# Graph attention on one core: VectorE's adds set singly between its other operations, registers loaded for 16 tiles, two quads weighted in any round, chunks of five at the end

## The reference, cut to what matters

```python
def _gatv2_layer(x, src, dst, edge_e, Wl, bl, Wr, br, att_w, bias):
    gl = (x @ Wl + bl).reshape(n, HEADS, CH)          # 4 heads of 32 channels
    gr = (x @ Wr + br).reshape(n, HEADS, CH)
    xj = gl[src]
    e = jax.nn.leaky_relu(xj + gr[dst] + edge_e, negative_slope=0.2)
    alpha = jnp.einsum('ehc,hc->eh', e, att_w)
    m = jax.ops.segment_max(alpha, dst, num_segments=n)
    alpha = jnp.exp(alpha - m[dst])
    denom = jax.ops.segment_sum(alpha, dst, num_segments=n)
    alpha = alpha / (denom[dst] + 1e-16)
    out = jax.ops.segment_sum(xj * alpha[..., None], dst, num_segments=n)
    return out.reshape(n, HEADS * CH) + bias
```

## Time and profile before

| | us |
|---|---|
| median of 3 runs | 7069.02 (7065.85 to 7079.0) |
| the profiled execution | 7070.88 |
| its span | 7069.1 |
| PE busy | 5523.2 (78%) |
| DVE busy | 4561.9 (65%) |
| POOL busy | 4643.2 (66%) |
| ACT busy | 2511.6 (36%) |
| mean granted clock of TensorE, as a share of 2.4 GHz | 0.901 |

### The profile page before, as it was taken

The page is one execution under the profiler, slowest core; times in us unless marked ns, Lnnn a source line. Parts: engine busy times, 40 slices in busy tenths (PEclk is TensorE's granted clock), DMA queues, the critical chain, the costliest instruction groups (busy, mean ns, idle before and its releaser), DMA issues.

```text
span 7069.1 us, 115934 instructions
## 1 busy us (share of the span) xinstructions
PE 5523.2 (78%) x33353; PEld 4640.2 (66%) x33353; DVE 4561.9 (65%) x15147; ACT 2511.6 (36%) x9678; POOL 4643.2 (66%) x4865
## 2 busy tenths in 40 slices
PE   7988871888888888788867878757877866888875
PEld 6655551787876587777556667656766765767764
DVE  5434321677676488777657777756777765777775
ACT  2554420777775387777401111110111111111111
POOL 1777776777774377777247777727777745777770
PEclk9999999999998599999679998978899987998986
DMA  3111112444443255444234444434444443444441
GB/s 105 42 41 36 40 23 67 130 125 128 125 128 80 73 154 149 145 146 140 41 103 137 138 133 138 132 58 134 135 136 134 138 93 95 138 136 135 138 129 22
DMA packets 396212, 763.44 MB, mean 108 GB/s; under 512 B 110888, under 2 KB 255133, under 8 KB 394825
## 3 DMA queue, kind: packets, MB, share of 16 engines
q0 software_dynamic: 180928, 315.57, 19.1%
q1 hardware_dynamic: 210314, 426.15, 17.9%
q10 hardware_dynamic: 4352, 14.30, 0.7%
HBM read 648.79 MB, written 106.03 MB: 107 GB/s over the span
## 4 chain that ended last, share of the span: by engine, by line
POOL 25%; DVE 11%; issue 11%; PE 10%; DMA 5%; DVEq 2%; ACT 1%; POOLq 0%; ACTq 0%
POOL AR L565 19%; POOL AR L557 6%; DMA AR<-gtab_d,AR 4%; PE PS L1313 3%; PE PS L1329 2%; DVE AR L1934 2%; PE PS L1326 2%; DVE AR L1950 2%; DMA AR<-ptab_d,AR 1%; DVE AR L1960 1%; DVEq L491 1%; DVE AR L1792 1%; DVEq L1934 1%; PE PS L1227 0%; DVE AR L1717 0%
## 5 line engine op out<-in xcount | busy, mean ns | idle before, releaser
L565 POOL DMA_INDIRECT AR<-gtab_d,AR x2436 | 2302.6, 945 | 1183.0 <-issue 706.9
L557 POOL DMA_INDIRECT AR<-ptab_d,AR x1624 | 1541.6, 949 | 684.9 <-issue 470.9
L1329 PE MATMUL PS<-AR,ident 128*128 128x140 f32 x4872 | 1199.4, 331 | 537.6 <-DMA AR<-gtab_d,AR 526.9
L1329 PEld LDWEIGHTS PS<-AR,ident 128*128 128x128 f32 x4872 | 849.6, 214 | 730.4 <-DMA AR<-gtab_d,AR 720.4
L1326 PE MATMUL PS<-AR 128*128 x4872 | 1108.0, 313 | 50.0 <-issue 49.3
L1934 DVE TENSOR_TENSOR AR<-AR,PS 112x132 f32 x2436 | 709.0, 291 | 579.1 <-DVE AR L1934 325.5
L542 POOL DMA_INDIRECT rec_d<-AR x782 | 790.0, 1010 | 387.9 <-issue 234.5
L1227 PE MATMUL PS<-AR,ident 128*128 128x160 f32 x3248 | 782.8, 323 | 268.0 <-DMA AR<-ptab_d,AR 263.3
L1326 PEld LDWEIGHTS PS<-AR 128*128 128x128 f32 x4872 | 858.5, 215 | 74.6 <-issue 73.6
L1010 ACT ACTIVATE AR<-AR 128x448 f32<-128x448 bf16 x609 | 332.4, 570 | 1601.2 <-PE PS L1313 1601.0
L1313 PE MATMUL PS<-AR 128*112 128x132 f32 x4872 | 805.8, 312 | 97.5 <-DVE AR L1934 86.6
(11 more groups left out here) (335 smaller groups left out, 8173.6 us busy)
## 6 DMA issues: line engine op xcount, KB each, us to landing
AR<-ste_d SPq DMA_DIRECT2D x404, 512.0 KB
AR<-nbb_d SPq DMA_DIRECT2D x303, 224.0 KB, 3.3
ste_d<-AR SPq DMA_DIRECT2D x101, 512.0 KB
AR<-gtab_d,AR POOLq DMA_INDIRECT x2436
AR<-ptab_d,AR POOLq DMA_INDIRECT x1624
nbb_d<-AR SPq DMA_DIRECT2D x101, 224.0 KB, 2.4
AR<-key_d SPq DMA_DIRECT2D x94, 224.0 KB
rec_d<-AR POOLq DMA_INDIRECT x782
```

The costliest lines, as they stand in the source:

```text
L557: e.indirect_dma_start(out=XJ1[:, t % 32, :], out_offset=None, in_=tabs_d[0][:, :], in_offset=off).then_inc(done_, 16)
L565: e.indirect_dma_start(out=xj2(t)[:, t % 4, :], out_offset=None, in_=tabs_d[1][:, :], in_offset=off).then_inc(done_, 16)
L1329: x = e.matmul(o, ident[:, :], xj2(t)[:, t % 4, :], start=False, stop=True, skip_group_check=True)
```

## The change

Four things are changed.

1. **Adds set singly.** `add()` takes one tile off a list and adds it. It stands between VectorE's other operations: after scans, carries and args have issued an operation whose result the next one needs, and around the weights, the terms and the scores. What is left is added at the end of the round. The list holds the quads weighted two rounds before, where it was one; the waits of the steps name the one operation that they need.
2. **Registers loaded for 16 tiles**, on VectorE and TensorE, in all five stages (255 loads an engine where there were 510).
3. **Two quads weighted in any round.** A chunk of eight is weighted in four rounds.
4. **Chunks of five at the end.** Chunks of eight up to quad 152, then nine of five and one of six (29 chunks), with steps one round apart from chunk 17 on. After round 202, again 11 quads are to be weighted; the last round is 213.

With more chunks the masks are built in every fourth round of the second message layer, the blocks' updates start in round 122, and SyncE's rule for loading masks follows STEPS.

```diff
-    ends = list(range(8, 193, 8)) + [196, 200, NQ]
+    ends = list(range(8, 153, 8)) + list(range(157, 198, 5)) + [NQ]
     px, steps, start = [], [], 0
     for c, end in enumerate(ends):
-        gap = 2 if c < 23 else 1
+        gap = 2 if c < 17 else 1
...
-            r = max(back + 1 - (c < 23), px[-1] if px else 0)
-            while px.count(r) >= (1 if r < NQ - 10 else 2):
+            r = max(back + 2 - gap, px[-1] if px else 0)
+            while px.count(r) >= 2:
...
-OWN = [{30 + 5 * b: b for b in range(NB)}, {136 + 2 * b: b for b in range(NB)}]
+OWN = [{30 + 5 * b: b for b in range(NB)}, {122 + 2 * b: b for b in range(NB)}]
...
-            g = t // 8
+            g = t // 16
             if cache.get("g") != g:
                 _, vs = nc.values_load_multi_w_load_instructions(
-                    BT[0:1, g * 8:g * 8 + half(g)], engines=[ENG[name]], min_val=0, max_val=NB,
+                    BT[0:1, g * 16:min(g * 16 + 16, T)], engines=[ENG[name]], min_val=0, max_val=NB,
                     skip_runtime_bounds_check_because="a sum of NB comparisons, so 0 to NB")
                 cache["g"], cache["v"] = g, vs
-            return cache["v"][t % 8]
+            return cache["v"][t % 16]
...
-                            if g8 == (5 * c + 11) // 2:
+                            if g8 == (4 * c + 11) // 2:
...
-                        if g8 == (4 * c + 4 if c < 24 else 100 + 2 * (c - 24)):
+                        if g8 == STEPS[c - 2][4] // 2 + 5:
...
-                    if l == 1 and j >= 2 and j % 5 == 2 and j // 5 < NCH:
-                        chunk_masks(j // 5)
+                    if l == 1 and j >= 2 and j % 4 == 2 and j // 4 < NCH:
+                        chunk_masks(j // 4)
...
+                def add():
+
+                    if not tiles:
+                        return
+                    t = tiles.pop(0)
+                    i, v_ = t // 4, t // 2
+                    c = chunk_of(i)
+                    if t == 4 * chunk_start(c):
+                        w.wait_ge(s_r, chunk_at(l, c))
+                        tb = max(t - 1, 0)
+                        _, (rb,) = nc.values_load_multi_w_load_instructions(
+                            BT[0:1, tb:tb + 1], engines=[ENG["vector"]], min_val=0, max_val=NB,
+                            skip_runtime_bounds_check_because="a sum of NB comparisons, so 0 to NB")
+                        o = ACC2[:, bass.ds(rb, 1), :, :]
+                        w.wait_ge(*acc_done_[0])
+                        acc_done_[0] = w.done(e.tensor_tensor(
+                            o, o, PS[4][0:B, 128:132].unsqueeze(1).unsqueeze(3).to_broadcast([B, 1, 4, 33]), ALU.mult), s_rs)
+                    w.wait_ge(s_scat2, pair_at(l, v_))
+                    w.wait_ge(*acc_done_[0])
+                    o = ACC2[:, bass.ds(block_of(cs, "vector", t), 1), :, :]
+                    x = e.tensor_tensor(o, o, PS[6 + v_ % 2][0:B, (t % 2) * 132:(t % 2 + 1) * 132].rearrange(
+                        "p (a h c) -> p a h c", a=1, h=4), ALU.add)
+                    acc_done_[0] = w.done(x, s_acc2 if t % 2 else None)
...
-                    v(e.tensor_tensor_scan(SR[:, ::-1], mk[:, 128:0:-1], PS[5][:, 127::-1], BIG, ALU.add, ALU.max))
-                    w.wait_own()
+                    both = v(e.tensor_tensor_scan(SR[:, ::-1], mk[:, 128:0:-1], PS[5][:, 127::-1], BIG, ALU.add, ALU.max))
+                    add()
+                    w.wait_ge(*both)
                     done(e.tensor_tensor(SS, SF, SR, ALU.max), s_s0)
...
-                    v(e.tensor_tensor(BE_, PS[5][0:1, 129:257], r[:, 256:384], ALU.add))
-                    w.wait_own()
-                    v(e.tensor_tensor(BL_.rearrange("p (h t) -> p h t", h=4), vr[:, :, 0:32],
-                                      r[:, 0:128].rearrange("p (h t) -> p h t", h=4), ALU.add))
+                    ends_ = v(e.tensor_tensor(BE_, PS[5][0:1, 129:257], r[:, 256:384], ALU.add))
+                    add()
+                    w.wait_ge(*ends_)
+                    lasts = v(e.tensor_tensor(BL_.rearrange("p (h t) -> p h t", h=4), vr[:, :, 0:32],
+                                              r[:, 0:128].rearrange("p (h t) -> p h t", h=4), ALU.add))
                     v(e.tensor_tensor_scan(GE_[:, ::-1], r[:, 511:383:-1], BE_[:, ::-1], BIG, ALU.add, ALU.max))
-                    w.wait_own()
-                    v(e.tensor_tensor_scan(GL_, r[:, 128:256], BL_, BIG, ALU.add, ALU.max))
-                    w.wait_own()
+                    w.wait_ge(*lasts)
+                    scanned = v(e.tensor_tensor_scan(GL_, r[:, 128:256], BL_, BIG, ALU.add, ALU.max))
+                    add()
...
+                def weight(i):
+
+                    t0 = 4 * (i - chunk_start(chunk_of(i)))
+                    w.wait_ge(s_r, chunk_at(l, chunk_of(i)))
+                    if i >= 5:
+                        w.wait_ge(s_scat2, pair_at(l, 2 * (i - 5) + 1))
...
+                    tiles = [4 * i + k for i in weighted_in(j - 2) for k in range(4)]
+                    quads = weighted_in(j)
                     for n, step in ((0, scans), (1, carries), (2, args)):
                         c = step_of(j, n)
                         if c is not None:
...
+                    add()
+                    if quads:
+                        weight(quads[0])
+                    add()
+                        terms(2 * j)
+                        add()
+                        terms(2 * j + 1)
+                        add()
+                        scores(j)
+                        add()
+                    if len(quads) > 1:
+                        add()
+                        weight(quads[1])
+                    while tiles:
+                        add()
```

More of the change, by code:

```diff
@@ L901, in scalar_program @@
                             done(e.activation(NBB[:, i % 8, :, :], SQB[:, i % 6, :, 0:B], ACT.Copy), s_nbx)
-                    if l == 1 and j >= 0 and j % 5 == 0 and j // 5 < NCH:
-                        c, t0 = j // 5, 4 * chunk_start(j // 5)
+                    if l == 1 and j >= 0 and j % 4 == 0 and j // 4 < NCH:
+                        c, t0 = j // 4, 4 * chunk_start(j // 4)
                         w.wait_ge(s_kx, c)
@@ L1188, in tensor_program @@
                         done(x, s_turn)
-                    if l == 1 and j >= 1 and j % 5 == 1 and j // 5 < NCH:
-                        c = j // 5
+                    if l == 1 and j >= 1 and j % 4 == 1 and j // 4 < NCH:
+                        c = j // 4
                         w.wait_ge(s_k4, c + 1)
@@ L1387, in v @@
             def v(inst):
-                w.done(inst)
+                return w.done(inst)
             def mile(inst, name):
@@ L1917, in add_quad @@
-                def add_quad(i):
-                    c = chunk_of(i)
-                    if i == chunk_start(c):
-                        w.wait_ge(s_r, chunk_at(l, c))
-                        t = max(4 * i - 1, 0)
-                        _, (rb,) = nc.values_load_multi_w_load_instructions(
-                            BT[0:1, t:t + 1], engines=[ENG["vector"]], min_val=0, max_val=NB,
-                            skip_runtime_bounds_check_because="a sum of NB comparisons, so 0 to NB")
-                        o = ACC2[:, bass.ds(rb, 1), :, :]
-                        w.wait_ge(*acc_done_[0])
-                        acc_done_[0] = w.done(e.tensor_tensor(
-                            o, o, PS[4][0:B, 128:132].unsqueeze(1).unsqueeze(3).to_broadcast([B, 1, 4, 33]), ALU.mult), s_rs)
-                    for v_ in (2 * i, 2 * i + 1):
-                        w.wait_ge(s_scat2, pair_at(l, v_))
-                        for t in (2 * v_, 2 * v_ + 1):
-                            w.wait_ge(*acc_done_[0])
-                            o = ACC2[:, bass.ds(block_of(cs, "vector", t), 1), :, :]
-                            x = e.tensor_tensor(o, o, PS[6 + v_ % 2][0:B, (t % 2) * 132:(t % 2 + 1) * 132].rearrange(
-                                "p (a h c) -> p a h c", a=1, h=4), ALU.add)
-                            acc_done_[0] = w.done(x, s_acc2 if t % 2 else None)
@@ new lines, in args @@
+                    columns = v(e.tensor_copy(CC, PS[5][:, 384:386]))
+                    add()
+                    w.wait_ge(*columns)
+                    once = v(e.scalar_tensor_tensor(SS, mk[:, 129:257], CC[:, 0:1], SS, ALU.add, ALU.max))
+                    add()
+                    w.wait_ge(*once)
+                    twice = v(e.scalar_tensor_tensor(SS, mk[:, 257:385], CC[:, 1:2], SS, ALU.add, ALU.max))
+                    add()
+                    w.wait_ge(*twice)
+                    done(e.tensor_tensor(SS, PS[5][:, 0:128], SS, ALU.subtract), s_arg)
@@ new lines, in terms, with scores @@
+                def terms(u):
+                    j, kk = u // 2, u % 2 * 2
+                    w.wait_ge(s_e, pair_at(l, u))
+                    if j >= 2:
+                        w.wait_ge(s_lin, quad_at(l, j - 2))
```

(27 more changed lines are left out.)

47 lines of the change are left out of this document (11 added, 36 removed).

## The result

The change takes 7017.28 us (7014.38 to 7022.29, four runs) where the kernel before takes 7067.44: a ratio of 0.9928, 95% interval 0.9911 to 0.9945. That is 50 us faster, and the forecast was 106.

What follows compares the result with a forecast made beforehand. GpSimd's unbroken gathers were taken to bound the kernel. Gains of 57.5 us on the lag and 49 on the tail, 106.5 together, bring 7070.9 to 6964.4, 6963 as the runs' median; range 6925 to 7030.

Steps and rivals of the forecast that it cites:

- The gathers set the pace: GpSimd issues gathers without a stop, 1013.95 us in the second layer, 5.0 us a quad; the change doesn't touch it.
- What an add costs: On VectorE, 0.45 us in a row, 0.21 with independent work on both sides; each taken from a row saves about 0.25.
- Eight quads in 35.5 of 40 us: Up to quad 152, VectorE's eight rounds take 35.5 us of the 40 us of gathers; 37.4 by the granted clock.
- lag: Last scores (round 202) behind the last gather: 31.5, 30.6, 37.4 us by layer before; forecast gain 57.5 us over three layers.
- the cover: Time the gathers leave over in a chunk of eight up to quad 152: 2.6 us in 40.
- A chunk of five 26.1 us: At a layer's end, each chunk of five takes 26.1 us against 25.0 us of gathers.
- lag 14 in each layer: At round 202: 4.7 us as at round 192 before, plus 9 from eight chunks; bounds 6 and 19.
- The tail 36: From the start of a layer's last scores to the end of its sums: 36 us, from about 52; bounds 33 and 42.
- Register loads "counted as nothing": Half of 510 loads, 0.6 us each on a queue, mostly hidden by gathers; 0 to 2 us a layer's end.
- Masks: Message layer: five masks in 20 rounds where four were, 3 us each; hidden by gathers, unhidden 3 us once.
- chunks of five don't keep up: Rival for a layer's end: 27.8 us a chunk, lag 27, tail 42, gain 49.5, 7020 us; chance 0.20.
- the slower case: Rival: waiting on adds lowers TensorE's mid-layer clock, loss from about granted 0.75; 7102 us in its example; chance 0.07.

Runs made afterwards that it cites:

- terms ahead of all sums: The change with TensorE's terms of both pairs queued before all sums in a round; 7036.72 us, 0.9955 of the kernel before.
- early switch: The change with one-round step gaps from chunk 8 on, not 17, and chunks of eight up to quad 192, then 5 and 6; 6982.78 us, 0.9889.
- the change's second run: The change itself, unedited, run again on the same chip as the kernel with registers loaded for eight tiles; 7015.49 us.
- late switch: The change with chunks of eight up to quad 192, then 5 and 6; one-round step gaps still start at chunk 17; 6987.57 us, 0.9867.
- terms between the sums: The late switch kernel with TensorE's order in a round two sums, both terms, two sums; 6980.61 us, 0.988 of the kernel before.

## Why the prediction was right or wrong

- **The gathers set the pace, and go on without a stop**: right. 1013.97 us against 1013.95, gaps of 0.3.
- **What an add costs** (0.21 with independent work on both sides, 0.45 in a row): right. In VectorE's timeline behind the scores of round 185 the last add shown starts 0.20 us before the next scores. The same stretch has the two waits that the prediction put at about 0.9 each, 0.79 and 0.76:

```profile
5685.86 0.45 DVE L1966 SCALAR_TENSOR_TENSOR AR<-PS,AR 128x280 f32<-128x280 f32 x1 [0.79 <-PE PS L1329]
5686.23 0.28 DVE L1886 TENSOR_TENSOR AR<-AR,PS 112x132 f32 x1
5687.26 0.45 DVE L1966 SCALAR_TENSOR_TENSOR AR<-PS,AR 128x280 f32<-128x280 f32 x1 [0.76 <-PE PS L1329]
5687.63 0.28 DVE L1886 TENSOR_TENSOR AR<-AR,PS 112x132 f32 x1
5687.83 0.73 DVE L1976 TENSOR_REDUCE AR<-AR 128x16 f32<-128x560 f32 x1
```

  The section on the change says that each add but the last of a round now has another operation before it. That is too much: of the 100 adds from 5600 to 5725 us, 37 still wait for the add or the rescaling before them, 6.9 us in all (the waits are shown with the terms ahead of all sums).

  The section of the Trainium skill that was weighed there ("VectorE: DVE Perf Modes", The DRAIN you can't avoid) says in its first paragraph that an operation which is not held back starts earlier; the prediction took the rule without this. Taken so, single adds would win nothing; the old table with single adds, at 0.9915, decides against it for these operations.
- **Eight quads in 35.5 of 40 us**: right as far as it can be seen. With eights to the end the second layer's lag goes from 9.8 at round 151 to 8.1, 5.8 and 4.7 at 159, 167 and 175. From 159 to 167 the chunk takes 37.8 us where its gathers take 40.1; at 175 the lag is as low as it gets. The early switch's third layer goes from 14.6 at round 87 to 5.2 at 119, 2.3 us a chunk, which gives the same. The estimate was 35.5 with TensorE at full clock and 37.4 with the granted one: the cover is thinner than the 2.6 us that were taken, but there.
- **A chunk of five 26.1 us**: right. From round 165 to 200, seven chunks, the lag grows by 7.6, 5.6 and 9.1 us, 1.06 each on average: 26.1. There is luck in it. In the change's second run it is 1.28, and with registers loaded for eight 0.34, so most of what a chunk of five takes over its gathers comes with the loads for 16. The sum has 0.5 us a chunk for loads and nothing for their new size.
- **"The eight chunks until round 202 then add 9 us to the 4.7 of the quiet part: lag 14 in each layer"**: this is the step that failed. It starts the fives from the quiet part's lag, and puts nothing for the way there: the switch to one-round gaps and then to fives. By the table, the quads whose adds have been made are 132 at round 148 and 154 at round 165: 22 quads in 17 rounds, with all the scores of 17 quads beside them. Lag went from 7.0 (mean of the layers) to 22.3 there, 15.3 us more; this is the term that the sum left out. It isn't the loads: with registers for eight it is 14.4. It is work brought forward (in the kernel before it is 131 to 148, 17 quads), and the forecast counted the lag that this work no longer makes in rounds 193 to 202 and not what it makes at 149 to 165. Up to round 157 the kernel with eights has the same rise, so that part is the one-round gaps'; it then works it off, and has 11.0 (mean) at round 165. The rest comes with the fives, the first of which follow before the rise is gone. How the 15.3 us divide between the two can't be said closely, since the lag swings by 6 to 11 us within a chunk of eight. Fives, at 1.06 us over their gathers each, can't work it off; eights can. Gain on the lag 7.9 where 57.5 was forecast.
- **The tail 36**: right, 36.1, 35.7 and 36.4; gain 48.7 of 49 forecast.
- **Register loads "counted as nothing"**: wrong, 16 us slower by the pair of runs. The step took half as many loads to be half the time. A load for 16 takes 1.10 us, not 0.6, and the waits for terms grow with it while VectorE is behind; by which chain stays open.
- **Masks**: nothing to be seen on the path. VectorE is busy 171.5 us of 200 in the message layer, where 175 was the estimate for a full stretch. The first gather came between 3586 and 3612 us over the runs of all kernels, 3597.8 before, too wide to tell 3 us from none.
- **Rivals**: "chunks of five don't keep up" gave 7020 us with a lag of 27, and 7017 came out, but by another way: its 27.8 us a chunk are not there, and its tail of 42 isn't either. The rival's time was right by luck and its mechanism wrong. The clock stayed at 0.91 in mid-layer and 0.80 at the end, so the slower case didn't come.

## What to carry to other kernels

Where a queue of work is moved forward to shorten a tail, add up its cost at the place that it is moved to, and ask whether anything behind that place runs faster than the bound: a backlog made at a switch lasts to the end when each later chunk takes just a little more than its budget. Before a schedule is made finer, split the change: single adds with the old table (and the loads for 16) won 60 us, the new table on top of them nothing, and single adds with eights to the end nearly 90. Fewer and larger register loads aren't cheaper by their count alone; look at how long one stops a queue, and at what the engines wait for in the rounds where one of them is behind, since sums over a whole layer hide it.

The fastest kernels run are the three with eights to the end (late switch, early switch, terms between the sums), at 0.987 to 0.989 of the time before, 30 to 37 us below the change. Eights, or the old table, together with registers for eight tiles weren't tried.

## What the runs showed of the hardware that wasn't expected

The same program took about 7070 us in some sets and 8794 in others, on the same two chips at different times. TensorE ran 580 matmuls from 300 to 500 us where it runs 1067, at a granted clock of 1.00 in both, and the other engines fell with it (GpSimd least, 120 instructions for 152); the ratio of the change to the kernel before went from 0.9928 to 1.0075. What slows the engines then was not found. A register load of 16 values takes 1.10 us in the middle against 0.60 for eight, which gives, as an estimate from these two points, about 0.06 us a value and 0.1 for the rest.
